# Attention and routed experts on one core: scores with their sign turned, row sums from a column of ones, and 2^14 applied where the probabilities are split

## The reference

```python
xn = _layernorm(x)                                     # (2, 2048, 256)
scores = einsum('bqe,bke->bqk', xn @ W_qk, xn) * SCALE
scores = scores + (kpos - qpos) * alibi_slope[0]
scores = where(causal, scores, -inf)
attn = softmax(scores, axis=-1)                        # exp(s - max s) / row sum
s = einsum('bqk,bkd->bqd', attn, xn @ W_v.T)
# experts: probs = softmax(xn @ Wr), one expert per token, at most 512 tokens each
h = maximum(xe @ W1[e], 0);  ye = h @ W2[e] * p_token
x = x + s * silu(y)
```

## Time and profile before

| | |
|---|---|
| median of 3 runs | 495.61 us (494.0 to 496.39) |
| the profiled execution, first to last instruction | 490.2 us |
| outside that span, against the median | 5.4 us |
| busy over the span | PE 440.0, DVE 353.6, ACT 257.8, POOL 223.5 us |
| chain that ended last, by engine | DVE 38%, PE 37%, ACT 11%, issue 5% |
| granted TensorE clock, mean | 0.985 |

### The profile page before, as it was taken

The page is one execution under the profiler, slowest core; times in us unless marked ns, Lnnn a source line. Parts: engine busy times, 40 slices in busy tenths (PEclk is TensorE's granted clock), DMA queues, the critical chain, the costliest instruction groups (busy, mean ns, idle before and its releaser), DMA issues.

```text
span 490.2 us, 8778 instructions
## 1 busy us (share of the span) xinstructions
PE 440.0 (90%) x3138; PEld 301.6 (62%) x3138; DVE 353.6 (72%) x953; ACT 257.8 (53%) x540; POOL 223.5 (46%) x336
## 2 busy tenths in 40 slices
PE   5686898999999879989998999999999999999960
PEld 2354565666577756666776777666666666666640
DVE  5879688687587768886766553788897979786340
ACT  1443453444544633545434545677686867768630
POOL 4107644332260372723031000348778687878761
PEclk9999998999999999999999999999999999999995
DMA  7982912702500485225001515328668474742140
GB/s 219 344 306 87 224 39 65 201 6 70 183 8 1 113 314 135 87 44 175 0 12 51 110 11 215 87 90 213 215 158 225 136 247 129 242 114 84 55 128 32
DMA packets 64315, 63.45 MB, mean 129 GB/s; under 512 B 36902, under 2 KB 58156, under 8 KB 62224
## 3 DMA queue, kind: packets, MB, share of 16 engines
q1 hardware_dynamic: 53472, 40.78, 29.0%
q0 software_dynamic: 5632, 16.73, 10.9%
q10 hardware_dynamic: 5168, 5.37, 3.3%
HBM read 30.29 MB, written 25.43 MB: 114 GB/s over the span
## 4 chain that ended last, share of the span: by engine, by line
DVE 38%; PE 37%; ACT 11%; issue 5%; POOL 3%; DMA 2%; SPq 1%; POOLq 0%; DVEq 0%; ACTq 0%
PE bank L1118 11%; PE bank L1120 11%; PE bank L1119 11%; DVE pmax L835 7%; DVE w_l L861 6%; DVE hid_l L879 4%; PE bank L1189 4%; ACT sc L1021 4%; DVE sc L804 3%; DVE pT_l L817 3%; ACT hid_h L1044 2%; DVE xnr L692 2%; ACT hid L1042 1%; ACT w_h L1033 1%; DVE stats L656 1%
## 5 line engine op out<-in xcount | busy, mean ns | idle before, releaser
L1027 ACT ACTIVATE pT_h<-bank 128x512 f16<-128x512 f32 (+2 forms) x80 | 42.1, 528 | 73.2 <-PE bank L1189 72.9
L1021 ACT ACTIVATE sc<-sc,nbias 128x512 f32<-128x512 f32 (+2 forms) x80 | 51.8, 648 | 48.1 <-DVE nbias L810 48.1
L1118 PE MATMUL bank<-v_h,pT_h 128*128 128x256 f16 x272 | 74.7, 275 | 0.9 <-DVE pT_l L817 0.9
L817 DVE TENSOR_TENSOR pT_l<-bank,pT_h 128x512 f16<-128x512 f32 (+2 forms) x80 | 48.4, 606 | 37.5 <-ACT pT_h L1027 37.5
L1120 PE MATMUL bank<-v_h,pT_l 128*128 128x256 f16 x272 | 74.7, 275 | 0.0
L1119 PE MATMUL bank<-v_l,pT_h 128*128 128x256 f16 x272 | 74.7, 275 | 0.0
L1118 PE MATMUL bank<-w_h,hid_h 128*128 128x256 f16 x256 | 69.8, 273 | 2.9 <-DVE w_l L861 2.8
L879 DVE TENSOR_TENSOR hid_l<-hid,hid_h 128x512 f16<-128x512 f32 x64 | 50.0, 789 | 29.7 <-ACT hid_h L1044 29.6
L1119 PE MATMUL bank<-w_l,hid_h 128*128 128x256 f16 x256 | 69.8, 273 | 0.0
L1120 PE MATMUL bank<-w_h,hid_l 128*128 128x256 f16 x256 | 69.8, 273 | 0.0
L1118 PE MATMUL bank<-xT,qT_h 128*128 128x512 f16 (+3 forms) x160 | 55.1, 348 | 8.8 <-DVE cmax L804 7.4
(11 more groups left out here) (170 smaller groups left out, 974.6 us busy)
## 6 DMA issues: line engine op xcount, KB each, us to landing
raw<-in_w_e SPq DMA_DIRECT2D x5, 2048.0 KB, 9.1
sc<-in_w_e SPq DMA_DIRECT2D x3, 2048.0 KB, 7.7
slots<-empty ACTq DMA_DIRECT2D x1, 4224.0 KB, 26.1
out<-xg SPq DMA_DIRECT2D x8, 512.0 KB, 3.3
rows<-xg SPq DMA_DIRECT2D x8, 512.0 KB, 4.1
rows<-so SPq DMA_DIRECT2D x8, 512.0 KB, 3.0
xg<-in_x SPq DMA_DIRECT2D x6, 512.0 KB, 4.6
xg<-in_x ACTq DMA_DIRECT2D x2, 512.0 KB, 5.8
```

The costliest lines, as they stand in the source:

```text
L817: v.tensor_tensor(pT_l[:, t % 2, cols], tr_ps[n % 2][:, 0:w], pT_h[:, t % 2, cols], ALU.subtract).then_inc(pT_lo, 1)
L1021: a_.activation(sc[:, k, cols], sc[:, k, cols], ACT.Exp, bias=nbias[:, k:k + 1], accum_out=psums[:, t % 3, c:c + 1]).then_inc(exp_made, 1)
L1027: a_.activation(pT_h[:, t % 2, c * GTOK:c * GTOK + w], tr_ps[n % 2][:, 0:w], ACT.Copy).then_inc(pT_hi, 1)
L1118: pe.matmul(ps, a_h, b_h, start=first, stop=False, skip_group_check=shared)
```

## The change

The score's factor changes sign, so `sc` holds the scores with their sign turned, and DVE takes the least value of a row instead of the largest. Then exp(score - max) is exp(-sc + min), and the least value is itself the exp's bias: `nbias` is gone. Where a tile has one chunk, that chunk's minimum is used as it stands, and a semaphore increment stands where the reduction was. The factor 2^14 is no longer in the exp; it is applied as the scale of the copy to `pT_h`, and by `scalar_tensor_tensor` instead of `tensor_tensor` for `pT_l`. The exp has no accumulator output. The row sum comes from TensorE: each block of `v_h` has a 257th column that GpSimd fills with ones once (a block is now 258 wide in memory), the two matmuls with `v_h` as the moving side take 257 columns, and DVE takes the reciprocal of the 257th column of the result in PSUM, after its wait for the values.

```diff
+P_UP = 2.0 ** 14
+VCOLS = D + 2
...
-        v_h = sb("v_h", [P, NG + 1, GT, D], F16)
+        v_h = sb("v_h", [P, NG + 1, GT, VCOLS], F16)
...
+        def least(t):
+            return cmin[:, t % 2, 0:1] if chunks(t) == 1 else rmin[:, t % 2:t % 2 + 1]
...
+            g_.memset(v_h[:, :, :, D:D + 1], 1.0).then_inc(consts_made, 1)
             g_.iota(bias[:, :], pattern=[[1, S]], base=P - S, channel_multiplier=-1,
...
             def score(t, c):
-                v.tensor_tensor_reduce(sc[...], sc_ps[n % 2][:, 0:w], bias[:, lo:lo + w],
-                                       score_mul[:, 0:1], -3e38, ALU.add, ALU.max, cmax[:, k, c:c + 1]
-                                       ).then_inc(score_read, 1)
+                last = v.tensor_tensor_reduce(sc[...], sc_ps[n % 2][:, 0:w], bias[:, lo:lo + w],
+                                              score_mul[:, 0:1], 3e38, ALU.add, ALU.min, cmin[:, k, c:c + 1])
+                last.then_inc(score_read, 1)
                 if c == chunks(t) - 1:
                     dve.wait_ge(score_read, n + 1)
-                    step(v.tensor_reduce(rmax[:, k:k + 1], cmax[:, k, 0:c + 1], AX.X, ALU.max))
-                    v.tensor_scalar(nbias[:, k:k + 1], rmax[:, k:k + 1], -1.0, LN2_UP, ALU.mult, ALU.add
-                                    ).then_inc(nbias_made, 1)
+                    if c:
+                        v.tensor_reduce(rmin[:, k:k + 1], cmin[:, k, 0:c + 1], AX.X, ALU.min
+                                        ).then_inc(least_made, 1)
+                    else:
+                        dve.sem_inc(least_made, 1)
             def low(t, c):
-                v.tensor_tensor(pT_l[:, t % 2, cols], tr_ps[n % 2][:, 0:w], pT_h[:, t % 2, cols], ALU.subtract
-                                ).then_inc(pT_lo, 1)
+                v.scalar_tensor_tensor(pT_l[:, t % 2, cols], tr_ps[n % 2][:, 0:w], P_UP, pT_h[:, t % 2, cols],
+                                       ALU.mult, ALU.subtract).then_inc(pT_lo, 1)
             def finish(t):
-                step(v.tensor_reduce(rsum[:, k:k + 1], psums[:, t % 3, 0:chunks(t)], AX.X, ALU.add))
-                step(v.reciprocal(rinv[:, k:k + 1], rsum[:, k:k + 1]))
                 dve.wait_ge(pv_full, t + 1)
+                step(v.reciprocal(rinv[:, k:k + 1], pv_ps[k][:, D:D + 1]))
...
-            v.tensor_scalar(score_mul[:, :], small_dn[:, 0:1], SM_SCALE * UNDO / X_UP, None, ALU.mult)
+            v.tensor_scalar(score_mul[:, :], small_dn[:, 0:1], -SM_SCALE * UNDO / X_UP, None, ALU.mult)
...
             def probs(t, cs):
-                    a_.activation(sc[:, k, cols], sc[:, k, cols], ACT.Exp, bias=nbias[:, k:k + 1],
-                                  accum_out=psums[:, t % 3, c:c + 1]).then_inc(exp_made, 1)
+                    a_.activation(sc[:, k, cols], sc[:, k, cols], ACT.Exp, bias=least(t), scale=-1.0
+                                  ).then_inc(exp_made, 1)
             def high(t, c):
-                a_.activation(pT_h[...], tr_ps[n % 2][:, 0:w], ACT.Copy
+                a_.activation(pT_h[...], tr_ps[n % 2][:, 0:w], ACT.Copy, scale=P_UP
...
             def values(t, c):
-                    last = product(pv_ps[t % 2][:, 0:D], pT_h[:, t % 2, rows_], pT_l[:, t % 2, rows_],
-                                   v_h[:, at, q, :], v_l[:, at, q, :], kb == 0, kb == t % NT)
+                    pe.matmul(pv_ps[t % 2][:, 0:D + 1], pT_h[:, t % 2, rows_], v_h[:, at, q, 0:D + 1],
+                              start=kb == 0, stop=False)
+                    pe.matmul(pv_ps[t % 2][:, 0:D], pT_h[:, t % 2, rows_], v_l[:, at, q, :], start=False, stop=False)
+                    last = pe.matmul(pv_ps[t % 2][:, 0:D + 1], pT_l[:, t % 2, rows_], v_h[:, at, q, 0:D + 1],
+                                     start=False, stop=kb == t % NT)
```

More of the change, by code:

```diff
@@ L176, in layer_kernel @@
         sc = sb("sc", [P, 2, S])
[L177 to L181, removed]
+        cmin = sb("cmin", [P, 2, NG])
+        rmin = sb("rmin", [P, 2])
         rinv = sb("rinv", [P, 2])
@@ L275, in layer_kernel @@
         score_read = sem("score_read")
-        nbias_made = sem("nbias_made")
+        least_made = sem("least_made")
         exp_made = sem("exp_made")
@@ L719, in _ @@
             norm_stats(1, range(GT))
-            dve.wait_ge(consts_made, 7 + NX)
+            dve.wait_ge(consts_made, 8 + NX)
             dve.wait_ge(small_turned, 1)
@@ L767, in unit @@
                     j = n - VAL
-                    v.scalar_tensor_tensor(v_l[:, at, j, :], a[:, 0:D], ACC_DOWN, v_h[:, at, j, :],
+                    v.scalar_tensor_tensor(v_l[:, at, j, :], a[:, 0:D], ACC_DOWN, v_h[:, at, j, 0:D],
                                            ALU.mult, ALU.subtract)
@@ L803, in score @@
                 dve.wait_ge(score_full, n + 1)
-                v.tensor_tensor_reduce(sc[:, k, c * GTOK:c * GTOK + w], sc_ps[n % 2][:, 0:w], bias[:, lo:lo + w],
-                                       score_mul[:, 0:1], -3e38, ALU.add, ALU.max, cmax[:, k, c:c + 1]
-                                       ).then_inc(score_read, 1)
+                last = v.tensor_tensor_reduce(sc[:, k, c * GTOK:c * GTOK + w], sc_ps[n % 2][:, 0:w],
+                                              bias[:, lo:lo + w], score_mul[:, 0:1], 3e38, ALU.add, ALU.min,
+                                              cmin[:, k, c:c + 1])
+                last.then_inc(score_read, 1)
                 if c == chunks(t) - 1:
                     dve.wait_ge(score_read, n + 1)
-                    step(v.tensor_reduce(rmax[:, k:k + 1], cmax[:, k, 0:c + 1], AX.X, ALU.max))
-                    v.tensor_scalar(nbias[:, k:k + 1], rmax[:, k:k + 1], -1.0, LN2_UP, ALU.mult, ALU.add
-                                    ).then_inc(nbias_made, 1)
+                    if c:
[3 more added lines that the diff above has]
+                        dve.sem_inc(least_made, 1)
             def low(t, c):
@@ L1009, in unit @@
                 else:
-                    a_.activation(v_h[:, at, n - VAL, :], a[:, 0:D], ACT.Copy, scale=ACC_DOWN).then_inc(hi_made, 1)
+                    a_.activation(v_h[:, at, n - VAL, 0:D], a[:, 0:D], ACT.Copy, scale=ACC_DOWN).then_inc(hi_made, 1)
                     if n == RANK - 1:
@@ L1017, in probs @@
                 k = t % 2
-                act.wait_ge(nbias_made, t + 1)
+                act.wait_ge(least_made, t + 1)
                 for c in cs:
                     cols = slice(c * GTOK, c * GTOK + chunk_blocks(t, c) * P)
-                    a_.activation(sc[:, k, cols], sc[:, k, cols], ACT.Exp, bias=nbias[:, k:k + 1],
-                                  accum_out=psums[:, t % 3, c:c + 1]).then_inc(exp_made, 1)
+                    a_.activation(sc[:, k, cols], sc[:, k, cols], ACT.Exp, bias=least(t), scale=-1.0
+                                  ).then_inc(exp_made, 1)
             def high(t, c):
@@ L1026, in high @@
                 act.wait_ge(turned, n + 1)
-                a_.activation(pT_h[:, t % 2, c * GTOK:c * GTOK + w], tr_ps[n % 2][:, 0:w], ACT.Copy
+                a_.activation(pT_h[:, t % 2, c * GTOK:c * GTOK + w], tr_ps[n % 2][:, 0:w], ACT.Copy, scale=P_UP
                               ).then_inc(pT_hi, 1)
@@ L1258, in turn_x @@
                     last.then_inc(x_turned, 1)
-            pe.wait_ge(consts_made, 7 + NX)
+            pe.wait_ge(consts_made, 8 + NX)
             warm_up(8)
```

1 line of the change is left out of this document (removed).

## The result

| | before | after |
|---|---|---|
| median | 495.51 us (4 runs, 494.0 to 496.39) | 486.23 us (4 runs, 485.52 to 487.92) |
| profiled execution, first to last instruction | 490.2 us | 484.6 us |
| mean granted TensorE clock in it | 0.985 | 0.982 |
| busy: PE, DVE, ACT, POOL | 440.0, 353.6, 257.8, 223.5 us | 441.1, 343.6, 251.5, 223.0 us |
| chain that ended last | DVE 38%, PE 37%, ACT 11% | PE 50%, DVE 29%, ACT 8% |

The ratio is 0.985 (0.981 to 0.988). The forecast was 489.0 us. The first thing to see is that the medians fell by 9.3 us and the spans of the two profiled executions by 5.6 only; the experiments tell which of the two is nearer to what the change is worth.

What follows compares the result with a forecast made beforehand. DVE and, behind it, ScalarE were taken to end TensorE's gaps, 24.1 us idle. Of 8.15 us taken from the chain 6.85 come out, less 0.25 for columns: 6.6, so 495.6 becomes 489.0 us, range 486.5 to 491.5.

Steps and rivals of the forecast that it cites:

- rsum: Row-sum reduction on DVE, 11 times on the chain: removing it saves 0.18 us each, 2.0 us.
- the reads: ScalarE's accumulator reads after the exps, 26 on the chain: removing them saves 0.09 us each, 2.3 us.
- The anchor: Median 495.61 us against a profiled span of 490.2 us: 5.4 us lie outside the span and stay.
- 20:79: Attention stage from 20 to 79 us of the trace: 1.85 of TensorE's 13.0 us idle goes.
- 158:193: Attention stage from 158 to 193 us of the trace: 1.55 of TensorE's 5.3 us idle goes.
- tiles of one chunk: Seven tiles on the chain lose rmax and nbias on DVE: 0.25 us each, 1.75 us; other bound 0.6.
- The columns: 544 value matmuls of 257 columns: 0.25 us added on TensorE, upper bound 2.0 us, lower bound nothing.
- A: Rival: the half-clock stretch at 79:83 goes too, 1.7 us more won, 487.3 us; chance 0.18.
- A second stretch at the lower clock: Sign of being wrong: TensorE runs at the lower clock in a second stretch; no size given.
- B: Rival: gain hidden by the next late links (ScalarE's copies, transposing DMA); 2.8 us come out, 493.1 us; chance 0.14.
- C: Rival: value matmuls lose pace from 257 columns and unaligned rows; a quarter more time gives 503.4 us; chance 0.05.
- D: Rival: the exp on ScalarE still drags a second instruction; 1.8 us fewer come out, 490.8 us; chance 0.05.

Runs made afterwards that it cites:

- sign_only: The whole change without the column of ones, so the accumulator's read and rsum stay as in the kernel before: 489.2 us, ratio 0.992.
- rowsum_only: The kernel before with only the row sums moved to the column of ones, nbias and the old split kept: 488.44 us, ratio 0.988.
- no_shortcut: The whole change, but tiles of one chunk keep the reduction of their minimum: 485.68 us, ratio 0.983 to the kernel before.
- whole_again: The changed kernel run again without an edit, beside the kernel before: 486.48 us, ratio 0.984.
- reads_kept: no_shortcut with the exp's accumulator output put back, its result unused: 488.83 us, ratio 0.989 to the kernel before.

## Why the prediction was right, point by point

**The size.** Forecast: 6.6 us off the kernel's own time. Measured at equal clock: 6.8 ± 0.5. The mechanism is the one forecast: nbias, rsum and the reads are gone, each part by itself shortens the kernel, and TensorE's idle time fell where it was said to. That the sum is as near as it is owes something to luck, as the terms show.

**The anchor was wrong, without harm.** "5.4 us lie outside the span": in the 59 executions of before whose span is on record it is 1.7. The profiled execution of before (0.985, 490.2 us) was among the quickest of their kind, and a time of 495.6 less 1.7 is a span of 493.9, just over the longest of them (493.7). So much of the other 3.7 us can be clock. That is not shown, and two things speak for something else beside it: three of the four runs (495.42 to 496.39) took longer than any of the 59 (495.4 at most), and in every later run the profiled execution is one of those timed, while here even the shortest, 494.0, would leave 3.8 us outside its span. Either way a change of 6.8 us moved the medians by 9.3, and that is why 486.2 lies 2.8 us under the forecast of 489.0.

**Stage by stage.** Idle gone, forecast and measured from the two traces: 20:79 1.85 and 1.6; 83:101 0.55 and 0.6; 101:117 0.2 and 0.2; 117:128 0.7 and 0.6; 158:193 1.55 and 1.1; 193:204.9 none and none; 204.9:270 2.0 and 1.7. Sum 6.85 and 5.8. 158:193, with tiles of one chunk, falls short most; 20:79, which has them too, falls short no more in proportion than 204.9:270, which has none. The rest of the way to 7.1 can't be laid to stages: the lower clock in 20:83 of the trace after hides some, and 0.4 us came after the attention's last value matmul (187.9 to 187.5 us from there to the end).

**The two halves.** What each was said to bring, and what it brings at equal clock when it is the first or the last to be made:

| part | forecast | made first | made last |
|---|---|---|---|
| sign, bias and shortcut (sign_only) | 3.2 | 3.3 ± 0.5 | 1.7 ± 0.75 |
| row sums (rowsum_only) | 3.4 | 5.35 ± 0.65 | 3.8 ± 0.7 |

3.3 and 3.8 make the 7.1 of the whole. The row sums alone bring 2 us more than forecast, and 1.5 ± 0.9 us can be had by either half. The forecast, which counted links on one chain, had neither, and the two nearly cancel: that is the luck. Why the shared part is just that large stays open. Inside the row sums, each made last, rsum is worth 1.8 ± 0.8 us and the reads 2.2 ± 0.75 (offered 2.0 and 2.3, 1.8 each to come out); together 7.25 - 3.3 = 4.0, just the sum of both.

**The mis-sized term: tiles of one chunk.** The prediction saves 0.25 us of DVE in each, for rmax and nbias together, with "I take nothing, as it moves no data" for the increment. From the accumulator's read to the next instruction it is 0.37 us before, 0.19 with nbias alone gone (no_shortcut) and 0.23 with both gone: 0.14 saved, as the wait and the increment hold DVE longer than the reduction whose place they take. 7 x 0.14 is 1.0 us in place of 1.75, between the two bounds named. On the way to the exp it is 0.49, 0.31 and 0.17, so there 0.32 is saved. The expectation of no_shortcut misread the term: nbias goes there too, so it tests only 0.25 - 0.18 = 0.07 a tile, 0.5 us in all, and 0 ± 0.7 can't tell that from nothing. The count was off as well. The chain of before passes nbias of five such tiles (22.95, 36.70, 41.14, 164.67 and 185.10 us) and 13 of the others, not 7 and 11, which changes the offer by 0.1 us.

**At no cost, rightly**: the scales on pT_h and the exp, the factor in pT_l (689 to 688 ns), rinv on PSUM (4 ns more behind the same reduction), its wait, and the memset: TensorE's first matmul starts at 3.33 us with it and 3.21 without, the first of the q matmuls at 16.2 to 16.75 with it and 16.0 to 16.7 without. **The columns** cost more than the 0.25 taken, 0.95 us by TensorE's pace, inside the bound of 2.0.

**The rivals.** A: the slow stretch did not go, the clock fell at two places (0.96 in 20:79, 0.74 in 79:83). "A second stretch at the lower clock" was named as a sign of being wrong. It came and says nothing of the change, for the kernel before has four in its second trace. What brings the falls is not shown. B: 6.8 us came out, not 2.5. C: 0.110 us apart, not 0.136, though its reason, rows off alignment, has something to it (0.7 us). D: no read of the accumulator is left. TensorE's idle time, 18.3 us here and 17.2 in whole_again, is a little above the 16 to 17 forecast.

## What to carry to other kernels

Read what one link costs from start to start of its neighbours, count it only where the chain passes and no further than the consumer's idle time in that stage: that gave 6.6 for 6.8 us, with two errors of 1.5 to 2 us that nearly cancel. Test parts both alone and last, for their gains need not add up. A wait and an increment are not free: here they held DVE for as long as the 128x1 reduction that they replaced. Before a time is predicted, look at the clock and span of all runs and not of the profiled one: the medians of one kernel lay between 492.7 and 494.9 us, at mean clocks of 0.978 and 0.971.

## Not expected of the hardware

- From the accumulator's read to the next DVE instruction: 0.23 us over a wait and an increment, 0.19 over the same wait and a whole 128x1 reduction that carries the increment.
- One kernel's executions spread over 4 us by the clock, which falls at other places in each: at 79 us in the first trace of before, near 26, 50, 81 and 186 in the second.
- Matmuls of 257 columns whose rows lie 516 bytes apart cost 10 ns a dozen more than their columns; of 264 columns and 528 bytes nothing more.
- Filling two gaps with matmuls left the clock as it was; 1.76 us of idle time ahead of the fall had stayed.
- Time less span is 1.73 us in kernels without the column of ones or with its value made on DVE, and in reads_kept; 2.05 in the others. The column is not its cause by itself, and nothing here shows what is.
